# Cross-attention two batches at a time, with split sums of the query exponentials

## The chip, the cores and the metric

One core of one Trainium2 chip runs the whole kernel. Its engines are TensorE (PE in the profile, its weight loads PEld), VectorE (DVE), ScalarE (ACT), GpSimd (POOL) and SyncE (SP), which issues the DMAs. The metric is the device time of one launch in microseconds (us).

## What is computed

One decoder layer over x and ctx, both 32 x 64 x 512 (batch, channel, position), float32: a self-attention over the channels, a cross-attention, and a feed-forward net (FFN) whose operands are rounded to 8-bit floats in groups of 32, each followed by a layernorm over the 512 positions. The change is in the cross-attention:

```
def _L0_xattn_ref(q, k, v, Wq, Wk, Wv, Wo, bo, g):
    DIM = 64
    HEADS = 8
    DIM_HEAD = 64
    ...
    qh = jnp.einsum('bcn,oc->bon', q, Wq).reshape(b, HEADS, DIM_HEAD, -1)
    kh = jnp.einsum('bcn,oc->bon', k, Wk).reshape(b, HEADS, DIM_HEAD, -1)
    vh = jnp.einsum('bcn,oc->bon', v, Wv).reshape(b, HEADS, DIM_HEAD, -1)
    qh = jax.nn.softmax(qh, axis=-2) * SCALE
    kh = jax.nn.softmax(kh, axis=-1)
    context = jnp.einsum('bhdn,bhen->bhde', kh, vh)
    out = jnp.einsum('bhde,bhdn->bhen', context, qh)
    out = out.reshape(b, HIDDEN, -1)
    out = jnp.einsum('bcn,oc->bon', out, Wo) + bo[None, :, None]
    norm = jnp.maximum(jnp.sqrt(jnp.sum(out * out, axis=1, keepdims=True)), 1e-12)
    return out / norm * g * np.sqrt(DIM)
```

The layer is x1 = layernorm(x + self-attention), x2 = layernorm(x1 + xattn(x1, ctx, ctx)), out = layernorm(x2 + FFN(x2)).

## The kernel before

**Stages.** Up to 97 us the first FFN weights and x are loaded and rounded; up to 213.7 us the self-attention runs beside the rest of the weights; from 213.7 to 801.7 us the cross-attention; then the FFN. x lies in `xt` as 16 token tiles (t) of two batches: partitions 0 to 63 hold the channels of one batch, 64 to 127 those of the other.

**Cross-attention, one batch per slot.** `slot(b, par, t)` of each engine works on batch b = 2t + par; a turn t is two slots. All products are float32 with a contraction of 128 partitions, which TensorE does as two instructions each, except the query logits.
- Key logits: `logits` (L1204) multiplies `WkT[:, par]`, whose other 64 rows are zero, with the ctx tile `ctxs`: four products of 512 columns per batch into banks 0 and 1.
- Query logits (L1211): `keep_x1`, four DMAs (`load_x1d`), `high_x1` on ScalarE and `split_x1` (L465) on GpSimd make of x1 a pair of 16-bit halves stacked over 128 partitions (`x1p`); two 16-bit products of 512 columns per block i against `Wq2`, four blocks per batch, into banks 4 and 5.
- VectorE `maxima`: the row maximum of the key logits (L705), the maximum of each head's 64 query logits (L709) and the subtraction into `EQ` (L712). ScalarE `exps`: exp of the keys out of the bank (L960, with the running sum read by a second short instruction) and of the queries in place (L963). `q_sum` (L718) sums each head's 64 exponentials, 512 columns an instruction, eight a turn; `q_recs` (L722) inverts them; GpSimd `norm_p` (L475) multiplies.
- TensorE transposes the key exponentials (`transpose_k`, L1223) and the query ones (`transpose_p`, L1234), 16 blocks each per batch, through banks 2 and 3; ScalarE copies them out (L873) into `ET` and `PTs`.
- `a_product` (L1240): ctx times the key exponentials, four products of 512 columns. Only half of the result's rows belong to the batch; ScalarE copies these to `ATs`. Then four products with `Bs` (L1301) and `scale_g` (L742) give `GTs`; `y_product` (L1247) is 16 products of 64 columns with `PTs` as the weights.
- y, position by channel: `bias_y` (L726), the square (L487), `sum_y` (L732), the power -1/2 (L489) and the product (L490); `transpose_y` (L1255, L1270) and `add_y` (L749) bring it back to channel by position and add it to x1.

**Order.** Each engine runs one list written out by hand; semaphores order the lists. TensorE's list carries the logits of batch b + 1 between the transposes and products of batch b. Middle turns are loops.

## Time and profile before

| | us |
|---|---|
| median of 3 runs | 1008.78 |
| the three runs | 1013.59, 1008.78, 1008.75 |
| span of the profiled execution | 1010.8 |
| cross-attention, first key product to first FFN product | 588.0 |
| one turn (two batches) in its middle | 35.5 |
| busy in one such turn: TensorE, VectorE, ScalarE, GpSimd | 34.9, 30.7, 24.1, 17.5 |

No other duration is given for the profiled execution than its span, which stands 2.0 above the median. A row of the timeline is start, duration, engine, line, operation, output <- input, count, and in brackets the idle time before it and what ended it. With several instructions in a row, the duration runs from the first start to the last end. Instructions of an engine overlap a little, so that what counts along a chain is the distance of two starts.

### The profile page before, as it was taken

How to read it: one execution, taken by the hardware profiler on the slowest of the kernel's cores; microseconds unless marked ns; L12 is line 12 of the kernel's file. 1: busy time of each engine (PE TensorE's matmuls, PEld its weight loads, DVE VectorE, ACT ScalarE, POOL GpSimd, SP SyncE). 2: the span in 40 equal slices, each digit the busy share in tenths (PEclk: the TensorE clock that was granted, in tenths of full speed). 3: DMA queues.
4: the chain of work that ended last, by engine and by line, in shares of the span. 5: the costliest groups of instructions: out<-in, count | busy, mean ns of one | idle time of the engine just before them, and what ended most of it. 6: DMA issues, size and time to landing. Idle time of an engine off the chain costs nothing.

```text
span 1010.8 us, 17612 instructions
## 1 busy us (share of the span) xinstructions
PE 809.3 (80%) x5463; PEld 545.3 (54%) x5463; DVE 759.0 (75%) x1660; ACT 568.5 (56%) x1051; POOL 437.1 (43%) x491
## 2 busy tenths in 40 slices
PE   2115555548999999999999999999999867778873
PEld 2104555524767676676766667676667633333331
DVE  3766777748788888888888888888888266666663
ACT  1119777636666666766666676666667223333332
POOL 4423333313445455454545545454553334444443
PEclk7557676659999999999999999999999789999997
DMA  8993111101001101101100110110010000000000
GB/s 201 204 200 137 32 31 31 37 21 32 14 19 31 22 9 31 31 1 30 31 21 10 31 31 0 31 31 21 10 31 1 1 1 30 23 21 21 21 21 31
DMA packets 30372, 38.77 MB, mean 38 GB/s; under 512 B 4496, under 2 KB 16784, under 8 KB 30352
## 3 DMA queue, kind: packets, MB, share of 16 engines
q1 hardware_dynamic: 30352, 38.51, 15.9%
q8 instruction: 12, 0.20, 0.1%
q14 instruction: 8, 0.07, 0.0%
HBM read 25.92 MB, written 4.19 MB: 30 GB/s over the span
## 4 chain that ended last, share of the span: by engine, by line
PE 58%; issue 14%; POOL 8%; DMA 8%; DVE 6%; ACT 5%; SPq 1%; POOLq 0%; ACTq 0%; DVEq 0%
PE bank L1247 11%; PE bank L1204 11%; PE bank L1240 11%; PE bank L1223 5%; PE bank L1170 5%; PE bank L1211 5%; ACT big L873 4%; PE bank L1234 4%; DMA big<-in_ctx_dram 4%; POOL big L545 3%; POOL rstd L540 3%; DMA big<-in_L_ffn_w_down_dram 2%; PE bank L1301 2%; DMA big<-in_L_ffn_w_up_dram 2%; DVE big L565 1%
## 5 line engine op out<-in xcount | busy, mean ns | idle before, releaser
L873 ACT ACTIVATE big<-bank 128x512 f32<-128x512 f32 (+4 forms) x368 | 195.3, 588 | 53.1 <-PE bank L1223 31.5
L475 POOL TENSOR_TENSOR big<-big 128x512 f32<-128x512 f32 x128 | 131.5, 1057 | 81.1 <-DVE big L722 81.1
L1204 PE MATMUL bank<-big,WkT 128*128 128x512 f32 x256 | 136.2, 614 | 13.0 <-DMA big<-in_ctx_dram 8.8
L873 ACT ACTIVATE big<-big 32x256 f32<-32x256 f32 (+6 forms) x160 | 120.3, 772 | 15.6 <-DVE big L766 9.9
L963 ACT ACTIVATE big<-big,q_scales 128x512 f32<-128x512 f32 x128 | 92.4, 722 | 64.3 <-DVE big L712 64.3
L960 ACT ACTIVATE big<-bank,big 128x512 f32<-128x512 f32 x128 | 87.7, 685 | 68.6 <-DVE big L705 67.5
L1247 PEld LDWEIGHTS bank<-big 128*128 128x128 f32 x1024 | 120.6, 194 | 5.6 <-DVE big L742 1.2
L1247 PE MATMUL bank<-big 128*128 128x64 f32 x1024 | 119.4, 275 | 1.0 <-DVE big L742 1.0
L1240 PE MATMUL bank<-big 128*128 128x512 f32 x256 | 116.7, 598 | 0.5 <-ACT big L873 0.5
L718 DVE TENSOR_REDUCE big<-big 128x8 f32<-128x512 f32 x128 | 87.1, 680 | 25.7 <-ACT big L963 24.7
L705 DVE TENSOR_REDUCE big<-bank 128x1 f32<-128x512 f32 x128 | 88.2, 689 | 17.5 <-PE bank L1204 14.4
L1170 PE MATMUL bank<-big 128*128 128x128 f32 x256 | 55.9, 407 | 54.5 <-ACT big L873 54.5
L712 DVE TENSOR_TENSOR big<-bank,big 128x512 f32<-128x512 f32 x128 | 88.5, 691 | 6.9
L709 DVE TENSOR_REDUCE big<-bank 128x8 f32<-128x512 f32 x128 | 87.0, 680 | 7.4 <-PE bank L1211 7.4
L465 POOL TENSOR_TENSOR big<-big 64x512 f16<-64x512 f32 x32 | 37.0, 1157 | 116.1 <-ACT big L873 116.0
L1073 ACT ACTIVATE big<-big,rstd 128x512 f32<-128x512 f32 x16 | 13.0, 812 | 125.1 <-POOL big L541 125.1
L1211 PE MATMUL bank<-Wq,big 128*128 128x512 f16 x256 | 76.7, 381 | 7.2 <-POOL big L465 7.2
L1170 PEld LDWEIGHTS bank<-big 128*128 128x128 f32 x256 | 51.6, 308 | 56.6 <-issue 32.9
L545 POOL TENSOR_TENSOR big<-big 128x1376 f32<-128x1376 f32 x16 | 40.1, 2508 | 93.5 <-DVE big L569 93.5
L1240 PEld LDWEIGHTS bank<-big 128*128 128x128 f32 x256 | 47.4, 190 | 54.3 <-issue 41.6
L1234 PEld LDWEIGHTS bank<-ident,big 128*128 128x128 f32 x512 | 59.7, 140 | 23.5 <-issue 16.9
L565 DVE TENSOR_REDUCE big<-big 128x43 f32<-128x1376 f32 (+2 forms) x42 | 46.6, 1109 | 31.1 <-DMA big<-in_L_ffn_w_down_dram 21.6
(116 smaller groups left out, 1406.1 us busy)
## 6 DMA issues: line engine op xcount, KB each, us to landing
big<-big SPq DMA_DIRECT2D x64, 128.0 KB, 2.3
big<-in_x_dram SPq DMA_DIRECT2D x2, 2048.0 KB, 17.3
big<-in_x_dram SPq DMA_DIRECT2D x4, 1024.0 KB, 11.2
xt<-in_x_dram SPq DMA_DIRECT2D x1, 4096.0 KB, 15.0
big<-in_ctx_dram SPq DMA_DIRECT2D x16, 256.0 KB, 2.7
out_dram<-big SPq DMA_DIRECT2D x16, 256.0 KB, 2.0
big<-in_L_ffn_w_down_dram SPq DMA_DIRECT2D x4, 688.0 KB, 6.7
big<-in_L_ffn_w_gate_dram SPq DMA_DIRECT2D x10, 256.0 KB, 2.7
```

Of the source, the lines that this page charges most:

```text
L475: pool.tensor_tensor(e, e, r, ALU.mult).then_inc(s.p_ready, 1)
L705: dve.tensor_reduce(kneg[:, par, i:i + 1], bank[i % 2][:], X, ALU.max, negate=True).then_inc(s.k_max_ready, 1)
L712: dve.tensor_tensor(EQ[:, par, i].rearrange("p (h d) -> p h d", d=DH), q, qmax[:, par, i].unsqueeze(2).to_broadcast([P, HEADS, DH]), ALU.s ...
L873: return act.activation(dst, src, ACT.Copy)
L960: act.activation(EK[:, par, i], bank[i % 2][:], ACT.Exp, bias=kneg[:, par, i:i + 1], accum_out=ksum[:, par, i:i + 1]).then_inc(s.k_exp_don ...
L963: act.activation(EQ[:, par, i], EQ[:, par, i], ACT.Exp, scale=q_scales[:, 1:2]).then_inc(s.q_exp_done, 1)
L1170: last = pe.matmul(bank[4 + 2 * k + a][:, P * l:P * l + P], qs[:, k, CL // 2 * a + l].rearrange("m h c -> m (h c)"), pd[:, k, CL // 2 * a ...
L1204: pe.matmul(bank[i % 2][:], WkT[:, par, P * i:P * i + P], ctxs, start=True, stop=True).then_inc(s.klog_ready, 1)
L1211: last = pe.matmul(bank[4 + i % 2][:], x1p[:, par, P * i:P * i + P], Wq2[:, part], start=(part == 0), stop=(part == 1))
L1234: last = pe.transpose(bank[2 + j % 2][:, P * i:P * i + P], EQ[:, par, i, P * j:P * j + P], ident[:])
L1240: return pe.matmul(bank[6][:], ctxT[:, i], ET[:, i], start=(i == 0), stop=(i == NT - 1))
L1247: last = pe.matmul(bank[6][:, C * i:C * i + C], PTs[:, j, P * i:P * i + P], GTs[:, j], start=(j == 0), stop=(j == NJ - 1))
```

## The change

The cross-attention now works on both batches of a tile at once; per turn, with f = t + 1:
- Query logits are float32 products of x1 straight from `xt` with `WqT`; key logits use `WkT[rows]`. Each product contracts over 64 partitions only, and the two batches' products lie on different halves of the array's rows (`rows = slice(C * par, C * par + C)`). The 16-bit halves, the four DMAs, `keep_x1`, `high_x1`, `split_x1` and the scaling of Wq in the set-up go; the set-up issues two small DMAs more.
- `a_product` and `y_product` write 64 partitions each, one batch per half of the array's columns. `y_product` has `GTs` as the weights and 512 columns of `PTs`: 8 products of 512 columns for 32 of 64. `g_product` is 16 products of 64 x 64 with 64 columns a turn, for 8 of 64 x 128 with 128.
- y comes out channel by position. The bias is added by ScalarE, the square by GpSimd, the sum over channels by TensorE (`sum_squares`), the clamp by VectorE, the power by GpSimd; TensorE spreads it (`spread_rn`), VectorE multiplies (`norm_y`), GpSimd adds to x1 (`add_y`).
- `fold_p` on GpSimd adds the upper 32 columns of each head's exponentials to the lower 32, both batches at once, four a turn; VectorE's `q_sum` then sums 32 columns per head for both batches at once, four a turn instead of eight, with a reciprocal each.
- Key and query logits share banks 0 to 3, all transposes banks 4 and 5, and the phases are apart: all key logits of f (beside the query transposes of t), then `y_product(t)`, then all query logits of f with the key transposes and `a_product` of f. The turns are written out, not looped.

```diff
+            def fold_p(f, i):
+                pool.wait_ge(s.q_exp_done, 8 * f + 2 * i + 2)
+                if f or i >= 2:
+                    pool.wait_ge(s.q_rec_ready, 4 * f + i - 1)
+                e = EQ[:, :, i].rearrange("p b (h d) -> p b h d", d=DH)
+                pool.tensor_tensor(qfold[:, i % 2], e[:, :, :, 0:DH // 2], e[:, :, :, DH // 2:DH], ALU.add
+                                   ).then_inc(s.q_folded, 1)
...
-            def q_sum(b, par, i):
-                dve.wait_ge(s.q_exp_done, 4 * b + i + 1)
-                ch.link(dve.tensor_reduce(qsum[:, par, HEADS * i:HEADS * (i + 1)],
-                                          EQ[:, par, i].rearrange("p (h d) -> p h d", d=DH), X, ALU.add))
...
+            def q_sum(f, i):
+                if f:
+                    dve.wait_ge(s.p_ready, 8 * f - 6 + 2 * i)
+                dve.wait_ge(s.q_folded, 4 * f + i + 1)
+                ch.link(dve.tensor_reduce(qsum[:, i], qfold[:, i % 2], X, ALU.add))
+                dve.reciprocal(qsum[:, i], qsum[:, i]).then_inc(s.q_rec_ready, 1)
...
+            def scale_g(t):
+                dve.wait_ge(s.k_exp_done, 8 * t + 8)
+                ch.link(dve.reciprocal(krec, ksum))
+                if t:
+                    dve.wait_ge(s.y_ready, t)
+                for par in range(2):
+                    dve.wait_ge(s.gt_ready, 2 * t + par + 1)
...
+            dve.wait_ge(s.g8_ready, 1)
+            for t in range(-1, T):
+                f = t + 1
+                front, back = f < T, t >= 0
                 if front:
...
+                    k_max(f, 0)
+                if t >= 1:
+                    norm_y(t - 1)
+                if back:
+                    scale_g(t)
                 if front:
...
+                    k_max(f, 1)
+                    ln_stats(xt[:, f, :], s.x1_var)
+                    k_max(f, 2)
+                    ln_apply(f, s.x1_rstd, s.x1_ready)
+                if t >= 1:
+                    x2_stats(t - 1)
                 if front:
...
+                    k_max(f, 3)
+                if t >= 1:
+                    ln_apply(t - 1, s.x2_rstd, s.x2_ready)
                     scale_x(t - 1)
                 if front:
...
+                    q_shift(f, 0)
+                    q_shift(f, 1)
+                    q_sum(f, 0)
+                if back:
+                    clamp_ss(t)
                 if front:
...
+                    q_shift(f, 2)
+                    q_sum(f, 1)
+                if t >= 1:
                     quantize_x(t - 1)
...
                 if front:
...
+                    q_shift(f, 3)
+                    q_sum(f, 2)
+                    q_sum(f, 3)
...
+            def exp_k(f, i):
+                if f and i == 0:
+                    act.wait_ge(s.tr_ready, 16 * f - 8)
+                    act.wait_ge(s.gt_copied, 2 * f)
+                for par in range(2):
+                    act.wait_ge(s.k_max_ready, 8 * f + 2 * i + par + 1)
+                    act.activation(EK[:, par, i], bank[2 * (i % 2) + par][:], ACT.Exp, bias=kneg[:, par, i:i + 1],
+                                   accum_out=ksum[:, par, i:i + 1]).then_inc(s.k_exp_done, 1)
...
+            for t in range(-1, T):
+                f = t + 1
+                front, back = f < T, t >= 0
+                for i in range(NT):
+                    if front:
+                        exp_k(f, i)
+                    if back:
+                        copy_p(t, i // 2, i % 2)
                 if front:
...
+                    act.wait_ge(s.ctxT_ready, f + 1)
+                    if f:
+                        act.wait_ge(s.at_ready, f)
                     copy(ctxT, bank[7][:].rearrange("p (i c) -> p i c", i=NT)).then_inc(s.ctxT_copied, 1)
+                if back:
+                    act.wait_ge(s.y_ready, t + 1)
+                    if t:
+                        act.wait_ge(s.x2_added, t)
+                    act.activation(Ysb, bank[6][:], ACT.Identity, bias=bo2[:, 0:1]).then_inc(s.y_biased, 1)
                 if front:
...
+                    for i in range(NT):
+                        exp_q(f, i)
+                        copy_k(f, i)
+                    act.wait_ge(s.at_ready, f + 1)
+                    if f:
+                        act.wait_ge(s.gt_ready, 2 * f)
+                    copy(ATs, bank[6][:]).then_inc(s.at_copied, 1)
...
+            def a_product(f, i):
+                if i == 0:
+                    pe.wait_ge(s.ctxT_copied, f + 1)
+                    if f:
+                        pe.wait_ge(s.y_biased, f)
+                pe.wait_ge(s.tr_copied, 16 * f + 2 * i + 2)
+                for par in range(2):
+                    rows = slice(C * par, C * par + C)
+                    last = pe.matmul(bank[6][rows, :], ctxT[:, i, rows], ET[:, par, i],
+                                     start=(i == 0), stop=(i == NT - 1))
+                if i == NT - 1:
...
+            def g_product(t):
+                pe.wait_ge(s.at_copied, t + 1)
+                if t:
+                    pe.wait_ge(s.y_normed, t)
...
+            for t in range(-1, T):
+                f = t + 1
+                front, back = f < T, t >= 0
                 if front:
...
+                    k_logits(f, 0)
+                    k_logits(f, 1)
+                if back:
+                    transpose_p(t, 0, 0)
+                    g_product(t)
                 if front:
...
+                    k_logits(f, 2)
+                if back:
+                    transpose_p(t, 0, 1)
                 if front:
...
+                    k_logits(f, 3)
+                if back:
+                    transpose_p(t, 1, 0)
+                    transpose_p(t, 1, 1)
                 if front:
...
+                    transpose_ctx(f)
+                if back:
+                    y_product(t)
+                if front:
+                    q_logits(f, 0)
+                    q_logits(f, 1)
+                    transpose_k(f, 0)
+                    transpose_k(f, 1)
+                if back:
+                    sum_squares(t)
+                if front:
+                    q_logits(f, 2)
+                    transpose_k(f, 2)
+                    a_product(f, 0)
+                    q_logits(f, 3)
+                    transpose_k(f, 3)
+                    for i in range(1, NT):
+                        a_product(f, i)
+                if back:
+                    spread_rn(t)```

TensorE, in the middle of a turn. The names are those of the section above: L1204 and L1211 key and query logits, L1247 `y_product`, L1223 key transposes. Before:

```order
L1204 MATMUL bank<-big,WkT 128x512 [waits k_exp_done]
L1211 MATMUL bank<-Wq,big 128x512 [waits q_shifted]
L1211 MATMUL bank<-Wq,big 128x512
L1247 MATMUL bank<-big 128x64 [waits pqT_copied,gt_copied]
L1247 MATMUL bank<-big 128x64 x15
L1223 MATMUL bank<-ident,big 128x128 [waits kT_copied]
```

Now (L1111 query transposes, L1119 the transpose of ctx, L1154 `y_product`, L1089 query logits):

```order
L1111 MATMUL bank<-ident,big 128x128 [waits tr_copied]
L1111 MATMUL bank<-ident,big 128x128 x3
L1119 MATMUL bank<-ident,big 128x128 [waits gt_copied]
L1119 MATMUL bank<-ident,big 128x128 x3
L1154 MATMUL bank<-big 64x512 [waits tr_copied,gt_copied]
L1154 MATMUL bank<-big 64x512 x7
L1089 MATMUL bank<-WqT,xt 128x512 [waits k_exp_done,x1_ready]
L1089 MATMUL bank<-WqT,xt 128x512
L1089 MATMUL bank<-WqT,xt 128x512 [waits k_exp_done]
```

The query logits stood ahead of `y_product`, beside the key logits; they now stand behind it, and it waits for the copies of all query transposes of its turn.

ScalarE, from the first key exponential of a slot or turn. L960 and L963 are the exponentials of keys and queries, L873 the copies. Before:

```order
L960 ACTIVATE big<-bank,big 128x512 [waits gt_copied,kT_ready,k_max_ready]
L963 ACTIVATE big<-big,q_scales 128x512 [waits q_shifted]
L960 ACTIVATE big<-bank,big 128x512 [waits k_max_ready]
L963 ACTIVATE big<-big,q_scales 128x512 [waits q_shifted]
L873 ACTIVATE big<-bank 128x512 [waits kT_ready] x2
L960 ACTIVATE big<-bank,big 128x512 [waits k_max_ready]
```

Now (L875 and L881 the exponentials of keys and queries, L792 the copies, L916 the bias of y):

```order
L875 ACTIVATE big<-bank,big 128x512 [waits k_max_ready,gt_copied,tr_ready]
L875 ACTIVATE big<-bank,big 128x512 [waits k_max_ready]
L792 ACTIVATE big<-bank 128x512 [waits tr_ready] x2
L875 ACTIVATE big<-bank,big 128x512 [waits k_max_ready] x2
L792 ACTIVATE big<-bank 128x512 [waits tr_ready] x2
L792 ACTIVATE big<-bank 128x512 [waits at_ready,ctxT_ready]
L916 ACTIVATE big<-bank,bo 128x512 [waits y_ready]
L881 ACTIVATE big<-big 128x512 [waits q_shifted] x2
```

Key exponentials took turns with query exponentials; now eight key exponentials and eight copies come first (the second and third pairs of each alike), then the bias, then the query exponentials. `gt_copied` on the first one was that of the batch before the last; it is now that of the turn just behind.

VectorE, at the end of a turn and the start of the next. L705, L709, L712 as above, L718 and L722 the sums and their reciprocal, L742 `scale_g`. Before:

```order
L742 TENSOR_TENSOR big<-bank,big 64x256 [waits gt_ready,dve_chain]
L742 TENSOR_TENSOR big<-bank,big 64x256
L718 TENSOR_REDUCE big<-big 128x8 [waits q_exp_done]
L722 RECIPROCAL big<-big 128x32 [waits dve_chain]
L705 TENSOR_REDUCE big<-bank 128x1 [waits klog_ready]
L709 TENSOR_REDUCE big<-bank 128x8 [waits qlog_ready]
```

Now (L662 and L663 the sums and reciprocals, L644 the key maxima, L686 `norm_y`, L667 and L672 `scale_g`):

```order
L662 TENSOR_REDUCE big<-big 128x16 [waits q_folded,p_ready]
L663 RECIPROCAL big<-big 128x16 [waits dve_chain]
L644 TENSOR_REDUCE big<-bank 128x1 [waits klog_ready] x2
L686 SCALAR_TENSOR_TENSOR big<-big,g,bank 128x512 [waits y_squared,rn_spread]
L667 RECIPROCAL big<-big 128x8 [waits k_exp_done]
L672 TENSOR_TENSOR big<-bank,big 128x256 [waits gt_ready,dve_chain]
```

`scale_g` moved from ahead of the last sum to behind the first key maxima of the next turn and `norm_y`; the sum waits for GpSimd's fold, not for ScalarE.

## Rows read from the trace of the kernel before

**Rows 1.** The page: span and busy times, engine by engine.

```profile
span 1010.8 us, 17612 instructions
...
PE 809.3 (80%) x5463; PEld 545.3 (54%) x5463; DVE 759.0 (75%) x1660; ACT 568.5 (56%) x1051; POOL 437.1 (43%) x491
```

**Rows 2.** Stretches: busy us and instructions of each engine, then granted clock, DMA share, GB/s.

```profile
core 0: us, PE busy (x) PEld busy (x) DVE busy (x) ACT busy (x) POOL busy (x), PEclk, DMA share, GB/s
213.70:801.70 588.00, 563.94 (x3201) 388.61 (x3202) 486.83 (x1032) 384.80 (x753) 276.04 (x331) 0.98 0.09 21
497.25:532.75 35.50, 34.89 (x200) 24.15 (x201) 30.68 (x67) 24.07 (x48) 17.48 (x22) 1.00 0.09 22
```

**Rows 3.** Timeline of TensorE in one turn.

```profile
497.25 1.12 PE L1204 MATMUL bank<-big,WkT 128*128 128x512 f32 x2 [0.60 <-DMA big<-in_ctx_dram]
...
500.81 3.68 PE L1247 MATMUL bank<-big 128*128 128x64 f32 x32
...
509.93 1.04 PE L1234 MATMUL bank<-ident,big 128*128 128x128 f32 x8
510.81 1.02 PE L1204 MATMUL bank<-big,WkT 128*128 128x512 f32 x2
511.67 0.59 PE L1211 MATMUL bank<-Wq,big 128*128 128x512 f16 x2
512.10 1.04 PE L1234 MATMUL bank<-ident,big 128*128 128x128 f32 x8
513.06 1.16 PE L1301 MATMUL bank<-Bs,big 64*128 64x128 f32 x8
...
532.75 0.69 PE L1204 MATMUL bank<-big,WkT 128*128 128x512 f32 x1 [0.61 <-DMA big<-in_ctx_dram]
```

**Rows 4.** Timeline of VectorE in the same turn.

```profile
511.87 0.69 DVE L705 TENSOR_REDUCE big<-bank 128x1 f32<-128x512 f32 x1 [0.79 <-PE bank L1204]
512.47 0.68 DVE L709 TENSOR_REDUCE big<-bank 128x8 f32<-128x512 f32 x1
513.19 0.69 DVE L712 TENSOR_TENSOR big<-bank,big 128x512 f32<-128x512 f32 x1
513.81 0.64 DVE L574 TENSOR_SCALAR big<-big 128x512 fp8e4<-128x512 f32 x1
```

**Rows 5.** Timeline of ScalarE in the same turn.

```profile
496.97 1.06 ACT L873 ACTIVATE big<-bank 128x512 f32<-128x512 f32 x2
...
508.31 0.69 ACT L960 ACTIVATE big<-bank,big 128x512 f32<-128x512 f32 x1 [2.26 <-DVE big L705]
508.89 0.19 ACT L960 ACTIVATION_READ_ACCUMULATOR big<-bank,big 128x1 f32 x1
509.63 0.72 ACT L963 ACTIVATE big<-big,q_scales 128x512 f32<-128x512 f32 x1 [0.55 <-DVE big L712]
```

**Rows 6.** GpSimd in the same turn by line: count, busy us, mean ns, idle before.

```profile
L475 POOL TENSOR_TENSOR big<-big 128x512 f32<-128x512 f32 x8 | 8.2, 1057 | 4.6 <-DVE big L722 4.6
```

**Rows 7.** Products on parts of the array in the set-up and the self-attention, and their stretches.

```profile
23.52 1.61 PE L1123 MATMUL bank<-wg_area 64*64 64x64 f32 x32 [0.47 <-ACT wg_area L873]
...
110.20 0.86 PE L1159 MATMUL bank<-big 128*32 128x32 f32 x64
...
23.40:24.90 1.50, 1.38 (x32) 1.38 (x32) 0.00 (x0) 0.07 (x1) 0.00 (x0) 0.50 0.93 363
110.10:111.20 1.10, 0.96 (x66) 0.74 (x64) 1.01 (x4) 0.77 (x2) 1.10 (x1) 0.84 0.00 0
```

**Rows 8.** TensorE: first products of the cross-attention, and the first of the FFN.

```profile
213.68 2.04 PE L1204 MATMUL bank<-big,WkT 128*128 128x512 f32 x2 [1.31 <-ACT wuT L873]
...
801.67 1.78 PE L1335 MATMUL bank<-wg_area,big 128*128 128x480 bf16 x4 [0.69 <-ACT big L873]
```

**Rows 9.** TensorE in the FFN: a gap, and the stretch behind it.

```profile
869.52 0.89 PE L1348 MATMUL bank<-ident_bf,big 128*128 128x128 bf16 x11 [2.58 <-ACT big L1056]
...
872.00:875.00 3.00, 3.00 (x9) 1.06 (x7) 1.39 (x4) 0.15 (x1) 1.43 (x1) 0.50 0.00 0
```

713 lines of the change are left out of this document (252 added, 461 removed).

## The prediction

> **What bounds the kernel now.** First the page: the span is 1010.8 us, and TensorE is the busiest engine [rows 1]. Then the busy times by stretch: the cross-attention takes 588.0 us, TensorE is busy in 563.9 of them, and its granted clock is 0.98; in one turn of two batches in its middle TensorE is busy for 34.9 of 35.5 us, while VectorE has 30.7, ScalarE 24.1, GpSimd 17.5 [rows 2]. Then TensorE's timeline of that turn: the only idle time is 0.6 us at the turn's start, for the ctx tile [rows 3]. So today a turn is the sum of TensorE's instructions, and what the other engines gain is worth nothing while that stays. The question is what TensorE's sum becomes, and whether the new order still lets one engine work while the others do.
>
> **TensorE's sum.** A float32 product of 512 columns takes 0.86 us (510.81 to 511.67), two 16-bit ones 0.43 (511.67 to 512.10), eight transposes 0.88 (509.93 to 510.81), eight instructions of the present G 1.16, 32 instructions of the present `y_product` 3.68 [rows 3]. New per turn, if products run one after another: key logits 8 x 0.86 = 6.9 (as now), query logits 6.9 (now 8 x 0.43 = 3.4), `a_product` 6.9 (as now), `y_product` 6.9 (now 2 x 3.5 = 7.0), 64 transposes 7.0 (as now), ctx 0.4, G 1.8 to 2.6, `sum_squares` 0.9 and `spread_rn` 1.7 (8 and 16 instructions at the transposes' 0.11), less the 4 transposes of y. That is 40 us, 5 more than now.
>
> But all the 512-column products now come in pairs on disjoint halves of the array. No row shows such a pair. The nearest are short products on parts of it [rows 7]: 64 instructions of 32 columns on four column groups start within 0.86 - 0.20 = 0.66 us, 10.5 ns apart, where the 0.43 us of 512 columns gives 27 ns for 32 alone; and 32 instructions of 64 x 64 and 64 columns take 1.6 us at half clock, 42 ns apart where 107 would be one after another. Both overlap by about 2.5. I take it that a pair costs as one (0.86); the bounds are 1.29 (the second starts when the first's first half is done) and 1.73 (none). With 0.86 the sum is 4 x 3.45 + 7.0 + 0.4 + 0.9 (G: the 1.6 at half clock, halved) + 0.9 + 0.9 = 24 us. The Trainium skill ("TensorE: Matmul & The Clock Gate", Part 3, packing small matmuls) states the same side: different tile positions run concurrently, four row tiles with 512 columns 3.07 times as fast; by that figure, an estimate, a pair is nearer 0.9 than 1.7. Rows 7 agree in kind.
>
> **VectorE, GpSimd, ScalarE.** VectorE loses four of eight sums of 512 columns (4 x 0.6, each step being 0.60 to 0.72 from start to start [rows 4]), the bias, one of two sums of y and the small memsets: 30.7 falls to about 27. GpSimd gains four folds at 1.05 us, the price of its 512-column product [rows 6], +4.2, loses the splits, and stays near 20. ScalarE stays at 22 to 24. So no engine needs more than 27 us, and by busy time alone the turn would fall. The halved sums are taken at nothing: they lie on an engine with 8 us to spare in the new turn.
>
> **What the new order makes of the turn.** The logits no longer cross the slots: the turn has a key phase and a query phase that hand over to each other, as the order of the three engines shows. I follow the chain round one turn, each step from start to start. A product pair is read 1.06 us after its start (510.81 to 511.87), a maximum takes 0.60, the query maximum 0.72 and its subtraction 0.62 (511.87, 512.47, 513.19, 513.81) [rows 3, 4]; a key exponential 0.58 with a read of 0.19 behind it, so 0.77 to 0.80 (at least 0.70, as neighbours overlap by 0.1); a query exponential 0.72, copies 0.5 apart [rows 5].
> 1. From the turn's first key product to ScalarE's first key exponential, which now waits for `scale_g` of the turn behind: 1.08 + two maxima 1.2 + `norm_y` 0.8 (G may not overwrite bank 7 before it) + G 1.0 + `scale_g` 0.5 = 4.6.
> 2. ScalarE's block, eight key exponentials and eight copies, because `y_product` waits for the last copy: 8 x 0.8 + 8 x 0.51 + 0.1 = 10.6. TensorE and VectorE mostly wait here.
> 3. `y_product`, which stands ahead of the query logits: 4 x 0.86 = 3.5.
> 4. From the first query product to the third: 1.08 + two maxima and subtractions 2.7, the exponential 0.7, two copies 1.15, four transposes 0.44, `sum_squares` 0.9 = 7.0.
> 5. From there to the next turn: 1.08, `q_shift` 2 2.64, a sum and its reciprocal 0.84, the rounding of x 1.26, `q_shift` 3 2.75, exponential and copies 1.8, the last part of `a_product` 0.87, `spread_rn` 0.9 = 12.15.
> Together 37.85 us. Behind VectorE's last subtraction the fold, the sum and `norm_p` of GpSimd (1.05 + 0.9 + 4 x 1.02) run beside TensorE's 7 us of transposes, products and the next key logits, and come in within a microsecond of them; the fold costs 0.2 a turn if it takes 1.3 instead of 1.05.
>
> Three corrections. The exponentials may be 0.1 shorter each: -0.4 as the middle. Where the tiling changes there is a gap of 0.09 us (512.10 + 0.88 to 513.06) [rows 3]; some seven such changes lie on the chain: +0.6. TensorE now idles several times a turn for 1.5 to 2.6 us, and behind a gap of 2.58 us in the FFN the granted clock of a stretch is 0.50, the lower level of 1.2 GHz [rows 9]. About 10.8 us of the chain are TensorE's; all at the lower level would cost +10.8. I take +0.55, a twentieth. **A turn of 38.6 us.** The Trainium skill ("TensorEngine Tiling (Array Packing)", Tiling Modes, key properties) says that a change of the tiling mode drains TensorE; that speaks against this order, which changes it some 17 times a turn, and the 0.09 us is what the trace shows of it.
>
> **The sum.** The first turn has a front only (23.3 us from key product to key product), the second is short (37.3), 13 more are full, and the last with the back behind it is 55.9: 116.5 + 13 x 38.6 = 618.3 us, and 1.3 to the first FFN product (the transposes and copy of x, as today). Today it is 801.67 - 213.68 = 588.0 [rows 8]. +31.6. The set-up loses VectorE's scaling of Wq but has two more DMAs ahead of the weights, and the first FFN turn waits for the last norm: -1 and +1. 1010.8 + 31.6 = 1042.4 by the profiled execution, which stands 2.0 above the median of the runs: **1040 us**.
>
> **Rivals.**
> - *TensorE's clock falls in the gaps* (slower still). For it: the gaps and the row of the FFN [rows 9]. Against: no gap exceeds 2.6, and today's attention holds 0.98. A quarter of TensorE's 10.8 us at the lower level: +2.7 a turn, 41.3, +75 to 85 us, about 1085. Chance 0.16.
> - *The pairs do not overlap* (the speed-up of the array is absent for long products): steps 1, 3, 4, 5 grow, the walk gives 45.9 a turn, 736 + 1.3 - 588 = +149, about 1157. Rows 7 speak against it. Chance 0.06. If they overlap by halves (1.29), the turn is 39.5 and the time 1067; that lies in my own case.
> - *The chain is shorter than I add it up* (faster). Its point of balance is a turn of 36.6, since the first turn no longer waits for the DMAs of x1's halves. ScalarE's block at 0.70 an exponential takes off 0.4 more, and 0.05 less at each of some 35 hand-overs 1.75: 38.6 - 0.55 - 0.4 - 1.75 = 35.9, 11 us less than now, about 997. For it: no engine is busy for over 27 us, so nothing but the waits holds the turn. Against: the hand-overs were read from rows. Chance 0.20, of which 0.03 for a turn at VectorE's 27 to 30 (900 to 940).
> - *The split sums matter, or don't happen as said*: if the fold and sum were in the chain the turn would gain or lose only 0.2 to 0.7; no case of its own.
>
> **How the numbers follow.** Forecast 0.50 (1018 to 1070), clock 0.16, no overlap 0.06, faster by over 0.5% 0.20, within 0.5% of today 0.08 (turns of 36.3 to 36.9). 0.5% is about what a measurement of this kernel can tell from no change. Slower: 0.50 + 0.16 + 0.06 = 0.72. The range is 995 to 1100: it leaves out no overlap, a few hundredths of the clock case above, and half of the faster case.
>
> **What would show it.** In the profile after: a turn of 37.3 to 39.5; TensorE busy for about two thirds of it, with idle time ahead of `y_product`, of the third key product and of the key transposes, ended by ScalarE; VectorE idle for some 7 us ahead of the first query maximum, ended by TensorE; ScalarE's eight exponentials and copies back to back over 10 us; two starts of a product pair a few tens of nanoseconds apart. Wrong would be: starts 0.86 apart (no overlap), 0.43 apart (half), a granted clock below 0.9 in the turns (the clock), or VectorE without its long gap (the chain is shorter).

## The result, and the profile after

| kernel | median, us | runs | ratio to the kernel before | 95% interval |
|---|---|---|---|---|
| before | 1011.18 | 1013.59, 1008.78, 1008.75, 1014.03 | | |
| after | 1063.98 | 1061.74, 1057.08, 1066.22, 1070.14 | 1.0519 | 1.0463 to 1.0575 |

Medians are over all runs of a kernel, ratios and intervals over the faster ones where its runs fall into two groups. The changed kernel is 5.2% slower: 53 us, where 29 to 32 were forecast. The rows of the page after (span; busy time; in 40 slices TensorE's busy tenths and granted clock; the chain of waits by engine):

```profile
span 1059.9 us, 15236 instructions
...
PE 732.5 (69%) x5249; PEld 421.5 (40%) x5264; DVE 681.0 (64%) x1396; ACT 505.3 (48%) x985; POOL 473.0 (45%) x474
...
PE   2115555587877777787787787787777778777774
...
PEclk9998767679899889889889899999998879999896
...
PE 32%; DVE 24%; ACT 16%; issue 14%; POOL 8%; DMA 4%; ACTq 1%; SPq 1%; POOLq 0%; DVEq 0%
```

Against [rows 1] TensorE does 77 us less and the kernel takes 49 more. The loss lies in the cross-attention. Its stretch now, beside [rows 2], and three of its turns (us, busy time of each engine, granted clock, DMA share, GB/s):

```profile
215.97:854.35 638.38, 491.46 (x3013) 265.38 (x3013) 407.98 (x775) 323.00 (x690) 314.56 (x317) 0.90 0.02 7
281.16:318.59 37.43, 28.62 (x191) 15.25 (x189) 25.11 (x49) 19.93 (x43) 19.46 (x21) 0.95 0.03 8
317.61:354.70 37.09, 27.29 (x191) 14.42 (x189) 24.99 (x50) 19.93 (x43) 19.32 (x21) 1.00 0.02 8
521.24:562.37 41.13, 31.81 (x191) 17.64 (x189) 26.32 (x49) 20.27 (x43) 20.19 (x21) 0.88 0.03 7
```

638.4 for 588.0 us is +50.4; the set-up is 2.3 longer and the FFN 3.6 shorter. The turns differ, though their instructions are the same. By TensorE's `spread_rn` the fourteen full turns take 37.4, 37.1, 42.5, 41.0, 41.0, 41.0, 41.1, 41.3, 38.0, 39.0, 37.6, 37.7, 37.8 and 41.7 us, at granted clocks of 0.95, 1.00, 0.84, 0.88 (five times), 0.96, 0.91, 0.95 (three times) and 0.85. Only the second has the full clock throughout, and seven of the fourteen lie below 0.9. TensorE in the first of the turns shown above; its gaps stand in brackets:

```profile
281.16 1.99 PE L1077 MATMUL bank<-big,WkT 64*128 64x512 f32 x8
283.08 1.09 PE L1111 MATMUL bank<-ident,big 128*128 128x128 f32 x8
284.41 0.69 PE L1143 MATMUL bank<-Bs,big 64*64 64x64 f32 x32 [0.24 <-DVE big L686]
287.58 1.13 PE L1077 MATMUL bank<-big,WkT 64*128 64x512 f32 x4 [2.48 <-ACT big L875]
288.64 1.09 PE L1111 MATMUL bank<-ident,big 128*128 128x128 f32 x8
...
295.58 3.65 PE L1154 MATMUL bank<-big 128*64 128x512 f32 x16 [1.31 <-ACT big L792]
299.16 1.99 PE L1089 MATMUL bank<-WqT,xt 64*128 64x512 f32 x8
...
304.26 1.14 PE L1100 MATMUL bank<-ident,big 128*128 128x128 f32 x8 [2.09 <-ACT big L792]
...
306.12 1.60 PE L1089 MATMUL bank<-WqT,xt 64*128 64x512 f32 x4
...
316.70 1.08 PE L1130 MATMUL bank<-big 128*64 128x512 f32 x4 [1.89 <-ACT big L792]
317.61 1.04 PE L1169 MATMUL bank<-ident,big 128*64 128x128 f32 x16
318.59 1.99 PE L1077 MATMUL bank<-big,WkT 64*128 64x512 f32 x8
```

Two pairs of 512-column products (x8, as each product is two instructions) start 1.92 us before what follows them (281.16 to 283.08), and one pair alone 1.06 us (287.58 to 288.64). So a further pair adds 0.86, the time of a single product [rows 3]: the pairs overlap fully. The 0.20 us that each group has beside its pairs lies at its two ends, where the tiling of the array changes. One row each of ScalarE and VectorE shows who waits for whom, the first key exponential (L875) for `scale_g` and the first query maximum (L651) for the query logits:

```profile
286.08 0.69 ACT L875 ACTIVATE big<-bank,big 128x512 f32<-128x512 f32 x1 [5.08 <-DVE big L672]
```

```profile
300.32 0.69 DVE L651 TENSOR_REDUCE big<-bank 128x8 f32<-128x512 f32 x1 [6.04 <-PE bank L1089]
```

Now the long turn, in rows of 3 us around its losses (same columns as above; the granted clock is the third number from the end):

```profile
524.24:527.24 3.00, 0.71 (x33) 0.59 (x32) 2.13 (x7) 1.08 (x3) 1.27 (x1) 1.00 0.00 0
527.24:530.24 3.00, 2.58 (x11) 1.67 (x12) 2.09 (x6) 2.90 (x9) 0.74 (x2) 0.71 0.00 0
...
542.24:545.24 3.00, 0.97 (x8) 0.73 (x8) 2.93 (x5) 1.74 (x4) 0.40 (x1) 1.00 0.00 0
545.24:548.24 3.00, 2.94 (x16) 2.94 (x16) 2.31 (x5) 2.48 (x6) 1.62 (x2) 0.56 0.00 0
548.24:551.24 3.00, 3.00 (x10) 1.49 (x11) 0.83 (x2) 0.14 (x1) 3.00 (x4) 0.50 0.00 0
```

Twice in this turn TensorE has little work (0.71 and 0.97 us in a row of 3), and as it has work again its clock falls to or towards the lower level of 1.2 GHz. The work there is on the chain. The clock does not fall behind every gap: the longest one of this turn, 2.95 us ahead of the last part of `a_product` (560.48), is followed by a clock of 1.00. The same anchors as the prediction's five steps, in both turns:

| step | forecast | turn at 281 | turn at 521 |
|---|---|---|---|
| 1: first key product to first key exponential | 4.6 | 4.92 | 4.92 |
| 2: ScalarE's block, to `y_product` | 10.6 | 9.50 | 10.46 |
| 3: `y_product` | 3.5 | 3.58 | 3.58 |
| 4: first to third query product | 7.0 | 6.96 | 8.27 |
| 5: to the next turn | 12.15 | 12.47 | 13.90 |
| sum | 37.85 | 37.43 | 41.13 |

Step 5 of the long turn holds one loss more, on VectorE. The rounding of x2 (L706) takes 0.69 us in the turn at 281 and 1.64 here, where it falls beside GpSimd's third fold (L436):

```profile
311.68 0.69 DVE L706 TENSOR_TENSOR big<-big 128x512 bf16<-128x512 fp8e4 x1
...
554.51 1.64 DVE L706 TENSOR_TENSOR big<-big 128x512 bf16<-128x512 fp8e4 x1
```

```profile
310.67 1.66 POOL L463 TENSOR_TENSOR big<-big,minus_half 128x8 f32<-128x8 f32 x1
...
554.06 1.54 POOL L436 TENSOR_TENSOR big<-big 128x512 f32<-128x512 f32 x1 [0.70 <-ACT big L881]
```

In the turn at 281 GpSimd is in its small power instruction then, and a fold takes 1.27 us. The Trainium skill ("SBUF — State Buffer", SBUF: two separate sides) says that a VectorE instruction with two SBUF inputs and a GpSimd instruction that reads SBUF exclude each other on a shared port pair, one waiting until the other is done. L706 has two SBUF inputs and the fold reads SBUF, and the trace agrees: L706 ends 0.55 us behind the fold (556.15 and 555.60), though it began in the fold's course, and grows by 0.95. What made the fold itself take 1.54 instead of 1.27 isn't shown.

### The profile page after: what moved, and what is told of

Same layout as the page of the kernel before. It is cut to its first block, busy times and chain, and to the rows that moved or that the text cites. A ratio compares the mean times of both kernels' runs of the same rounds, so it can differ in the third digit from the quotient of the medians.

```text
span 1059.9 us, 15236 instructions
## 1 busy us (share of the span) xinstructions
PE 732.5 (69%) x5249; PEld 421.5 (40%) x5264; DVE 681.0 (64%) x1396; ACT 505.3 (48%) x985; POOL 473.0 (45%) x474
## 2 busy tenths in 40 slices
PE   2115555587877777787787787787777778777774
## 4 chain that ended last, share of the span: by engine, by line
PE 32%; DVE 24%; ACT 16%; issue 14%; POOL 8%; DMA 4%; ACTq 1%; SPq 1%; POOLq 0%; DVEq 0%
ACT big L792 10%; DVE big L651 6%; PE bank L1154 5%; PE bank L1040 5%; PE bank L1077 5%; ACT big L875 5%; PE bank L1089 4%; DVE big L654 4%; DVE big L527 3%; POOL big L510 3%; POOL rstd L505 3%; DMA big<-in_L_ffn_w_down_dram 2%; PE bank L1111 2%; PE bank L1100 2%; PE bank L1130 2%
## 5 line engine op out<-in xcount | busy, mean ns | idle before, releaser
L792 ACT ACTIVATE big<-bank 128x512 f32<-128x512 f32 (+3 forms) x352 | 188.5, 600 | 39.1 <-PE bank L1130 19.9
L651 DVE TENSOR_REDUCE big<-bank 128x8 f32<-128x512 f32 x128 | 87.3, 682 | 113.9 <-PE bank L1089 113.9
L881 ACT ACTIVATE big<-big 128x512 f32<-128x512 f32 x128 | 80.6, 630 | 142.8 <-DVE big L654 142.8
L445 POOL TENSOR_TENSOR big<-big 128x512 f32<-128x512 f32 x128 | 133.2, 1068 | 0.0
L875 ACT ACTIVATE big<-bank,big 128x512 f32<-128x512 f32 x128 | 87.8, 705 | 83.7 <-DVE big L672 78.4
L436 POOL TENSOR_TENSOR big<-big 128x512 f32<-128x512 f32 x64 | 83.7, 1308 | 88.5 <-ACT big L881 88.5
L644 DVE TENSOR_REDUCE big<-bank 128x1 f32<-128x512 f32 x128 | 82.0, 682 | 51.5 <-PE bank L1077 51.5
L1100 PE MATMUL bank<-ident,big 128*128 128x128 f32 x512 | 86.7, 323 | 35.7 <-ACT big L792 35.3
L1077 PE MATMUL bank<-big,WkT 64*128 64x512 f32 x256 | 79.6, 726 | 40.0 <-ACT big L875 38.7
L1100 PEld LDWEIGHTS bank<-ident,big 128*128 128x128 f32 x512 | 66.7, 163 | 87.4 <-ACT big L792 61.5
L1130 PE MATMUL bank<-big 128*64 128x512 f32 x256 | 67.8, 630 | 36.8 <-ACT big L792 36.8
L792 ACT ACTIVATE big<-big 32x256 f32<-32x256 f32 (+4 forms) x112 | 90.3, 834 | 1.1
L1111 PE MATMUL bank<-ident,big 128*128 128x128 f32 x512 | 78.4, 301 | 7.2 <-ACT big L792 6.8
L1111 PEld LDWEIGHTS bank<-ident,big 128*128 128x128 f32 x512 | 60.7, 152 | 51.8 <-ACT big L792 23.1
L1089 PE MATMUL bank<-WqT,xt 64*128 64x512 f32 x256 | 79.1, 718 | 0.3 <-ACT big L875 0.3
L457 POOL TENSOR_TENSOR big<-big 128x512 f32<-128x512 f32 x16 | 16.6, 1038 | 134.9 <-ACT big L916 134.9
L1040 PEld LDWEIGHTS bank<-big 128*128 128x128 f32 x256 | 52.8, 314 | 56.5 <-issue 40.1
L1154 PE MATMUL bank<-big 128*64 128x512 f32 x256 | 58.5, 597 | 20.4 <-ACT big L792 20.4
```

Of the source, the lines that this page charges most:

```text
L445: pool.tensor_tensor(e, e, r, ALU.mult).then_inc(s.p_ready, 1)
L651: ch.link(dve.tensor_reduce(qmax[:, i, par], q, X, ALU.max))
L792: return act.activation(dst, src, ACT.Copy)
L875: act.activation(EK[:, par, i], bank[2 * (i % 2) + par][:], ACT.Exp, bias=kneg[:, par, i:i + 1], accum_out=ksum[:, par, i:i + 1]).then_inc ...
L1040: last = pe.matmul(bank[4 + 2 * k + a][:, P * l:P * l + P], qs[:, k, CL // 2 * a + l].rearrange("m h c -> m (h c)"), pd[:, k, CL // 2 * a ...
L1077: pe.matmul(bank[2 * (i % 2) + par][:], WkT[rows, P * i:P * i + P], ctxs[rows, f % 2], start=True, stop=True).then_inc(s.klog_ready, 1)
```

## The experiments

The theory after this reading: a turn is the chain of hand-overs, some 37 us at full clock (the turn at 317.61 above), and the falling clock adds some 2.5 on the average. Rivals: the chain is the wrong one (shortening a hand-over then brings nothing); the clock is a companion of the slow turns and not their cause; the split sums cost or gain what the words of the change suggest. To compare, one number was read in each trace: the fourteen full turns, from the first to the fifteenth `spread_rn`. The first row is the kernel after, 39.6 us a turn; the rows of the others follow where they are discussed.

```profile
280.19:834.52 554.33, 425.71 (x2634) 230.43 (x2632) 360.54 (x688) 281.38 (x602) 278.96 (x282) 0.91 0.02 7
```

**The fold undone.** GpSimd adds nothing, and VectorE sums 64 columns.

```diff
-                dve.wait_ge(s.q_folded, 4 * f + i + 1)
-                ch.link(dve.tensor_reduce(qsum[:, i], qfold[:, i % 2], X, ALU.add))
+                dve.wait_ge(s.q_exp_done, 8 * f + 2 * i + 2)
+                e = EQ[:, :, i].rearrange("p b (h d) -> p b h d", d=DH)
+                ch.link(dve.tensor_reduce(qsum[:, i], e, X, ALU.add))
...
```

> The fold of GpSimd is taken out again: VectorE sums all 64 columns of each head for both batches, 1024 columns an instruction. Theory (a chain of hand-overs round the turn; the split sums lie beside it): the second sum of a turn stands on the chain and grows from 0.7 to about 1.25 us, +0.5 a turn; VectorE's last rounding instruction, 1.64 us beside GpSimd's fold in the turns of 41 us and 0.69 in those of 37.5, may go back to 0.69. 1050 to 1072 us. Rival (the fold and its extra hand-over, or its load on GpSimd, make the kernel slow): at least 1.5 us less a turn, below 1040.

Measured: 1080.42 us, ratio 1.0703 (1.066 to 1.0746); turns of 38.9 to 42.7. That is 16 us slower than after and above every expectation. The split sums are not the loss; they are a gain. Whether the unsteady clock makes it larger (1.2 us a turn between these two traces) can't be told from one trace each; a later run measures them at a held clock.

**Query logits ahead of `y_product`.** Steps 3 and 4 of the chain: VectorE gets its first query maxima while TensorE is in `y_product`.

```diff
+                if front:
+                    q_logits(f, 0)
+                    q_logits(f, 1)
                 if back:
                     y_product(t)
                 if front:
-                    q_logits(f, 0)
-                    q_logits(f, 1)
                     transpose_k(f, 0)
```

> TensorE's first two groups of query logits stand ahead of y_product instead of behind it; nothing else changes. Theory: y_product's 3.6 us leave the chain for VectorE's first maxima, and ScalarE's first query exponential comes some 1.5 to 2 us earlier: a turn shorter by 2.1 us (walk of the chain), about 1030, 1015 to 1045 with the clock. Rival (TensorE's own work sets the turn): no change, 1055 or more.

Measured: 1012.43 us, ratio 0.996 (0.9914 to 1.0007), no difference from the kernel before that can be told: 52 us, the whole loss, came back for two lines in another place. That is a little below the expected 1015 to 1045.

```profile
273.52:783.10 509.58, 408.42 (x2634) 214.41 (x2632) 356.36 (x687) 277.41 (x602) 273.73 (x281) 0.94 0.03 7
```

The turn falls by 3.2 to 36.4 us. That is more than the 2.1 expected of the hand-over itself; the granted clock rose from 0.91 to 0.94 as well. The clock was under-estimated in the gain as in the loss.

**The reciprocals of the key sums at the turn's end.** In the kernel after, VectorE inverts the key sums at the next turn's start, so ScalarE's next key exponentials, whose running sums go to the same place, wait for `scale_g` (step 1). Here the reciprocal stands at the turn's end with a semaphore of its own.

```diff
-                dve.wait_ge(s.k_exp_done, 8 * t + 8)
-                ch.link(dve.reciprocal(krec, ksum))
+                dve.wait_ge(s.krec_ready, t + 1)
...
+                    dve.wait_ge(s.k_exp_done, 8 * f + 8)
+                    if f:
+                        dve.wait_ge(s.gt_copied, 2 * f)
+                    dve.reciprocal(krec, ksum).then_inc(s.krec_ready, 1)
...
-                    act.wait_ge(s.gt_copied, 2 * f)
+                    act.wait_ge(s.krec_ready, f)
```

> The reciprocal of the key sums is taken at the end of the turn, so that ScalarE's first key exponential of the next turn waits for it and no longer for scale_g. Theory: step 1 of the chain, 4.6 us from the first key product to the first key exponential, falls to about 2; ScalarE's block starts some 3 us earlier, of which 1.7 to 3 stay: 1015 to 1040. Rival (ScalarE's block is not on the chain): no change, 1055 or more.

Measured: 1034.76 us, ratio 1.0241 (1.02 to 1.0282): inside the expectation. Where the clock is 1.00 a turn takes 35.2 us, 1.8 less than after; in between lie turns of 40.2 at 0.87. Both hand-overs are on the chain. The mean of the fourteen turns fell by 1.5 only, to 38.1, with the clock at 0.91 as in the kernel after.

**TensorE kept busy.** Thirteen products of 256 columns that nobody reads, at four places where TensorE stood idle; nothing else moves.

```diff
+            def keep_busy(b, n, semaphore, value):
+                pe.wait_ge(semaphore, value)
+                for _ in range(n):
+                    pe.matmul(bank[b][:, 0:256], ident[:], ident[:].unsqueeze(1).to_broadcast([P, 2, P]),
+                              start=True, stop=True)
...
+                if front and back:
+                    keep_busy(6, 3, s.gt_copied, 2 * t + 2)
...
+                        if back and i == NT - 1:
+                            keep_busy(7, 4, s.y_ss, t + 1)
```

> After's kernel with 13 products a turn (256 columns of the identity, 0.43 us each) put into TensorE's idle time at four places, into banks that nobody reads; work is only added. Theory (the turns of 41 us are those in which TensorE's clock falls to 1.2 GHz in the gaps): granted clock above 0.95 in the turns, all turns 37.4 to 38.5, 1030 to 1045 us. Rival (the long turns come from another cause, such as VectorE and GpSimd colliding): the turns of 41 us stay, 1058 or more.

Measured: 1022.34 us, ratio 1.0119 (1.0088 to 1.0151).

```profile
275.72:793.50 517.78, 464.96 (x2999) 265.66 (x2996) 350.87 (x685) 279.40 (x602) 271.24 (x280) 1.00 0.03 7
```

TensorE does 39 us *more* work in these turns and they are 36.5 us shorter, each 37.0 at a clock of 1.00. The kernel after takes as long, 37.1, in its one turn at full clock, where nothing was added; so the unread products change the turn by nothing but the clock that they hold. The time is below the expected 1030 to 1045, since no turn is longer than the shortest expected. So the clock costs 42 of the 53 us, with what follows from it, and the other 11 are what the chain costs at full clock: a turn takes 37.0 us against the 35.5 of the kernel before, and the whole cross-attention 600.2 against 588.0, as what lies outside the fourteen turns is some 9 us shorter. VectorE's busy time falls by 9.7 although its list is untouched, 6.6 of it in L706, which no longer meets a fold (14 times 692 ns on the average, 1166 in the kernel after).

**Both moves.** The second and the third edit together.

> Both orders of before at once: first query logits ahead of y_product, and the reciprocal of the key sums at the end of the turn. Theory (chain of hand-overs): the two lie on different steps of the chain, so they add up, some 3.8 us a turn off at full clock (33.5 us a turn), and the granted clock again below 1 in some turns: 960 to 1000 us. Rival (an engine's work becomes the bound at about 35 us): no faster than the better of the two, 1000 to 1015.

Measured: 980.83 us, ratio 0.9652 (0.9596 to 0.9708), the first version that beats the kernel before. Turns take 33.0 us at a clock of 1.00 and up to 37.1 at 0.87; the profiled execution was the slowest of the four (991.69), so its mean of 35.0 is above that of the others. At full clock the reciprocals give 1.8 and the query logits, on top of them, 2.2 (37.0, 35.2, 33.0). The two add up as expected, and the result is inside the 960 to 1000.

**Both moves, and TensorE kept busy at four places** (twelve products).

> The same with 12 unread products a turn in TensorE's idle time (256 columns of the identity, 0.43 us each). Theory: clock 1.00 in all turns, a turn of 33.5 to 34 us, 15 x 3 to 3.5 us less than the kernel with the unread products alone (1022): 965 to 980. Rival (the unread products now stand in the way, since the gaps are shorter): slower than the same kernel without them.

Measured: 1000.06 us, ratio 0.986 (0.9816 to 0.9903). Missed: the clock is 1.00, yet every turn takes 35.4. TensorE shows why:

```profile
566.03 1.56 PE L1181 MATMUL bank<-ident 128*128 128x256 f32 x6 [0.95 <-DVE big L672]
567.53 1.13 PE L1081 MATMUL bank<-big,WkT 64*128 64x512 f32 x4
...
575.67 1.13 PE L1181 MATMUL bank<-ident 128*128 128x256 f32 x4
576.74 3.65 PE L1158 MATMUL bank<-big 128*64 128x512 f32 x16
```

The unread products (L1181) wait for VectorE's `scale_g` (L672), and the third key product stands behind them in the queue; with both moves it no longer had to wait for that. It comes 6.39 us after the turn's first (561.14) instead of 3.87, and the first query product 1.3 us later than with both moves alone; the two unread products ahead of `y_product` (575.67), another place where TensorE no longer waits, add the other 1.1. A filler sits on the chain as soon as the wait that it filled is gone.

**Both moves, and unread products at two places only**, two behind the bias of y and four behind `y_ss`, where idle time was left.

> The run with both moves (query logits ahead of the y product, reciprocals of the key sums at the turn's end), with six unread 256-column products on TensorE at two places only: two behind the bias of y, four behind the root of the squares, both at points where TensorE stood idle in that run's trace. Its turns were 33.0 us at a granted clock of 1.00 and 37.1 at 0.87. Theory (the clock is what stretches its turns, and the twelve unread products of the run before it lay partly on the chain, ahead of the third key product, which these six don't): every turn at 1.00 and 33.0 to 34.0 us, 16 turns some 30 us shorter than with the clock unsteady, so 955 to 975 us. Rival (any product in the gaps comes into the chain's way, or the clock falls all the same): 980 us or more, turns of 35 us or at clocks under 0.95.

Measured: 962.66 us, ratio 0.9505 (0.946 to 0.955), all turns 33.0 to 33.1:

```profile
272.50:735.07 462.57, 417.76 (x2803) 228.64 (x2801) 352.38 (x685) 276.28 (x602) 272.92 (x280) 1.00 0.03 8
```

**TensorE kept busy at two of the four places** in the kernel after.

> Unread products at two of the four places alone (three ahead of the third key products, four between the first and second key transposes); the gaps ahead of y_product (1.3 us) and of the last part of a_product (1.9 to 3.0) stay. Theory (every gap counts for the clock by its length): a part of the 42 us, 1025 to 1050, granted clock between 0.94 and 0.98 in the turns. Rival (the last gap alone lets the clock fall): 1055 or more.

Measured: 1031.72 us, ratio 1.0172 (1.0122 to 1.0223), turns of 37.0 to 38.6 at clocks of 1.00 to 0.96. Two filled gaps, those ahead of the third key product and behind the first key transposes, give back most of it: 32 of 42 us. The length of one gap doesn't decide it: that of 2.48 us ahead of the third key product is followed by 1.00 in the turn at 281 and by 0.71 in the turn at 521.

**The fold undone at a held clock.** The first edit together with the thirteen unread products.

> The split sums undone (VectorE sums 64 columns, no fold) with 13 unread products a turn as in the kernel of 1022 us; the clock is thus held and only the sums differ. Theory (the longer sums stand on the chain between q_shift 2 and q_shift 3 and ahead of the last norm_p): turns alike, 0.5 to 1.5 us longer than 37.0, 1030 to 1046. Rival (undoing the split costs time only through the clock): within 5 us of 1022.

Measured: 1031.92 us, ratio 1.0183 (1.0136 to 1.0229), all turns 37.5.

```profile
277.03:802.35 525.32, 464.94 (x2999) 265.69 (x2997) 379.49 (x686) 279.43 (x602) 209.48 (x225) 1.00 0.02 7
```

Against the run with the fold, VectorE has 28.6 us more in fourteen turns (four sums of 1.20 instead of 0.68), GpSimd 61.8 less, and a turn is 0.5 us longer, 7.5 us over the fourteen; the medians differ by 9.6, the ratios by 0.6% (the two were measured beside different runs of the kernel before). The split sums are worth 0.5 us a turn where the order gives GpSimd room.

**The kernel before with the fold alone.** One batch and one tile at a time, in the old order.

```diff
+            def fold_p(b, par, i):
+                pool.wait_ge(s.q_exp_done, 4 * b + i + 1)
+                e = EQ[:, par, i].rearrange("p (h d) -> p h d", d=DH)
+                pool.tensor_tensor(qfold[:, par, i], e[:, :, 0:DH // 2], e[:, :, DH // 2:DH], ALU.add
+                                   ).then_inc(s.q_folded, 1)
...
-                dve.wait_ge(s.q_exp_done, 4 * b + i + 1)
+                dve.wait_ge(s.q_folded, 4 * b + i + 1)
...
```

> The kernel before with one part of the change alone: GpSimd adds the 32-column halves of each head's query exponentials, one batch and one tile at a time, and VectorE sums 32 columns. Nothing else moves. Theory (a slot of the kernel before is bound by TensorE, rows 7, and what VectorE gains and GpSimd loses lies in their idle time; GpSimd's four folds of some 0.65 us each stand in front of its products with the reciprocals): within 1% of the kernel before, 1002 to 1022 us. Rival A (the split sum is a gain by itself also there): under 1000 us. Rival B (GpSimd's folds delay the high and low parts and the normalised exponentials that TensorE waits for): 1025 us or more.

That TensorE bounds a slot stands in [rows 2], not in rows 7. Measured: 1051.72 us, ratio 1.0388 (1.0339 to 1.0436). The theory, that it changes nothing, was wrong; the time is that of rival B. The chain of waits by engine, and VectorE's sums, GpSimd's folds and ScalarE's key exponentials by line, with the sums and the exponentials of the kernel before behind them:

```profile
POOL 30%; issue 29%; PE 10%; ACT 10%; DVE 9%; DMA 8%; SPq 3%; POOLq 1%; ACTq 0%; DVEq 0%
...
L739 DVE TENSOR_REDUCE big<-big 128x8 f32<-128x256 f32 x128 | 53.7, 420 | 122.6 <-POOL big L474 122.1
L474 POOL TENSOR_TENSOR big<-big 128x256 f32<-128x256 f32 x128 | 94.7, 740 | 69.5 <-ACT big L983 69.5
...
L980 ACT ACTIVATE big<-bank,big 128x512 f32<-128x512 f32 x128 | 87.7, 685 | 131.1 <-DVE big L726 130.6
```

```profile
L718 DVE TENSOR_REDUCE big<-big 128x8 f32<-128x512 f32 x128 | 87.1, 680 | 25.7 <-ACT big L963 24.7
...
L960 ACT ACTIVATE big<-bank,big 128x512 f32<-128x512 f32 x128 | 87.7, 685 | 68.6 <-DVE big L705 67.5
```

Each sum is 0.26 us shorter (420 ns against 680), 33 us in all. But VectorE now waits 122 us for the folds, at a place in its queue where the sums waited 26 before. What stands behind them in the queue comes later, the key maxima too: ScalarE's key exponentials wait 131 us for these, 69 before, and TensorE for ScalarE. The chain runs through GpSimd's list, whose folds stand between its products with the reciprocals, the square of y and the low halves of x1. So rival B's time came by another road in the main: the folds hold up VectorE's queue more than GpSimd's own results. One turn:

```profile
499.99:538.08 38.09, 35.88 (x201) 23.80 (x200) 28.72 (x66) 23.61 (x48) 23.22 (x29) 1.00 0.09 21
```

38.1 us against 35.5 [rows 2], at a clock of 1.00. Whether the folds and sums, placed elsewhere in the two lists, would win that back wasn't tried.

**More hand-overs shortened**, by five more moves on top of both: the first key transposes also ahead of `y_product`, the third query product ahead of `sum_squares`, the third `q_shift` ahead of `clamp_ss`, ScalarE's first query exponential and first copy ahead of the bias of y, and the first fold ahead of the square. TensorE's part of the edit, against the run with both moves:

```diff
                     q_logits(f, 0)
                     q_logits(f, 1)
+                    transpose_k(f, 0)
                 if back:
                     y_product(t)
                 if front:
-                    transpose_k(f, 0)
                     transpose_k(f, 1)
+                    q_logits(f, 2)
                 if back:
                     sum_squares(t)
                 if front:
-                    q_logits(f, 2)
```

> The run with both moves, and four hand-overs of the turn shortened further: the first transpose of the key exponentials also ahead of the y product; the third query product ahead of the sums of squares; on ScalarE the first query exponential and the first copy ahead of the bias of y; on VectorE the shift of the third query maxima ahead of the sums of the tile before; on GpSimd the first fold ahead of the square of y. Theory (a turn is the chain of hand-overs, and each of these is a step of it): 31.0 to 32.5 us a turn where the clock is 1.00, 1 to 2 us less than with both moves alone; with the clock unsteady as there, 940 to 975 us. Rival A (the turn is then bound by the sum of TensorE's own work, some 29 us at full clock, and the later bias of y delays the A product): turns of 33 us or more at 1.00, 975 us or more. Rival B (shorter gaps keep the clock at 1.00 as well): all turns near 32, 925 to 945 us.

Measured: 944.37 us, ratio 0.932 (0.9276 to 0.9365). Inside the expected 940 to 975. Turns take 31.4 us, every third one or so 32.8 at a clock of 0.95. How the 1.6 us divide among the five moves wasn't taken apart. The fourteen turns, and two that follow each other with the gap at the end of each:

```profile
271.06:716.38 445.32, 384.37 (x2634) 201.99 (x2632) 352.32 (x687) 279.07 (x602) 271.74 (x281) 0.98 0.03 8
302.45:333.85 31.40, 26.99 (x191) 14.19 (x188) 25.14 (x50) 19.93 (x43) 19.40 (x21) 1.00 0.04 9
333.85:366.62 32.77, 28.61 (x191) 14.96 (x189) 25.17 (x50) 19.93 (x43) 19.40 (x21) 0.95 0.02 9
```

```profile
332.94 1.08 PE L1138 MATMUL bank<-big 128*64 128x512 f32 x4 [2.58 <-ACT big L797]
...
365.71 1.08 PE L1138 MATMUL bank<-big 128*64 128x512 f32 x4 [2.57 <-ACT big L797]
```

Both turns have the same three gaps of over 0.6 us (0.94, 0.65 and 2.58). Behind the one at 332.94 the clock falls for a while, which is the 0.95 of the turn that begins there; behind its like at 365.71 the next turn runs at 1.00.

**The same with six unread products** at the two places.

> The run with the four further hand-overs shortened, and six unread 256-column products of TensorE at two places: two behind the bias of y, ahead of the third transpose of the key exponentials, four behind the root of the squares, ahead of the last A product. Theory (the chain at a held clock): all turns 31.5 to 33 us at 1.00, 925 to 955 us. Rival (with so little idle time left, unread products cost what they take, 0.11 us each at full clock and their waits): equal to or slower than the run without them, by up to 20 us.

Measured: 939.9 us, ratio 0.9289 (0.9241 to 0.9337), all turns 31.4 to 31.5 at 1.00. The interval overlaps that of the run without them, so no gain is shown by the times; the two traces differ by 4.6 us over the fourteen turns (445.32 against 440.69), but the clock had little left to give. An unread product takes 0.5 us (four in 1.99), not the 0.11 of the expectation. It is the fastest kernel of the study, 6.6 to 7.6% below the kernel before and 12% below the one after.

## Why the prediction was right, and where its size was not

**Slower, for the reason given: shown.** TensorE's sum fell from 34.9 us a turn to 27.3 where the clock is 1.00 (24 forecast; that sum left out the changes of tiling), VectorE's to 25 and ScalarE's to 20 (27 and 22 to 24 forecast), and no engine is busy for over 32 of 41; the turn is a chain through all engines. Two of its hand-overs, undone one by one, gave 2.2 and 1.8 us a turn at a clock of 1.00.

**The pairs overlap.** A further pair adds 0.86 us, as taken (1.92 for two, 1.06 for one), and the changes of tiling add the 0.2 beside a group of pairs. The rival without overlap is out, and so is the half overlap of 1.29.

**The five steps, without the clock.** The turn at full clock is 37.0 us (TensorE kept busy), where the forecast without its 0.55 for the clock was 38.05. In that run the five steps take 4.92, 9.51, 3.58, 6.96 and 12.01. The forecast was 1.05 too long, by step 2: ScalarE's eight exponentials and copies took 9.5 us instead of 10.6, since neighbours overlap (two exponentials start 0.66 to 0.68 apart, where 0.8 was taken). Steps 1, 3, 4 and 5 came within 0.32. VectorE's gap ahead of the query maxima is 6.0 us (forecast 7).

**The term that was mis-sized is the clock.** "I take +0.55, a twentieth" stands in the prediction for what the gaps do to TensorE's 10.8 us on the chain. Measured: 39.6 - 37.0 = 2.6 us a turn, the size of the rival (2.7) that had a chance of 0.16; and by the prediction's own sign for that rival, a clock below 0.9 in the turns, it came true in seven of fourteen. That the time still fell between 1018 and 1070 is in part luck, as the two errors stand against each other: 14 turns x (2.05 - 1.05) = +14 us, and the first two turns, 65.2 us instead of 60.6, are the 19 us between the forecast 619.6 and the measured 638.4. With the steps as long as forecast, 1.05 us more a turn, and the clock as it was, the time would have been some 15 us longer than 1064, above 1070. The argument against the rival was that today's attention holds 0.98 and that no gap exceeds 2.6 us. The first is true but doesn't bear on it: today's turn has one gap of 0.6, and the new one has five of over 0.6 us. The second holds at full clock (2.48 is the longest gap), not in the long turns, where the slower work makes one of 2.96. The row of the FFN [rows 9] showed the case, and was given a twentieth.

**The loss of clock spreads.** The forecast priced TensorE's own work only. In the long turns L706 takes 0.95 us more as well, because it meets the third fold. That VectorE and GpSimd hold each other up was in none of the steps.

**The split sums.** "Taken at nothing" in the busy sum, and 0.2 to 0.7 a turn if on the chain: measured 0.5. The fold took 1.27 to 1.31 us for the 1.05 taken.

**The ends.** The first two turns took 25.4 and 39.8 us (23.3 and 37.3 forecast) at clocks of 0.83 and 0.87; with TensorE kept busy they take 25.5 and 36.9, so the excess of the second is the clock again, and that of the first is not explained. The first key product came 2.3 us later (forecast 1 earlier), the FFN was 3.6 us shorter (forecast 1 longer); neither was followed up.

## What to carry over

When a new order takes work off a busy engine and turns its sum into a chain of hand-overs, write down the chain, and then price TensorE's part of it at both clock levels: four gaps of 1.3 to 3.0 us in a turn cost here 42 of 1064 us through the clock, and shortening the hand-overs gave that back along with the steps. Before the bound is accepted, look for products that wait in the queue behind work that nobody needs yet: two such moves turned +5.2% into -3.5%, five more into -6.8%. And a reduction made shorter by a helper on another engine is only shorter where its queue doesn't stand waiting for the helper.

## What the runs showed of the hardware

- Products that nobody reads, six or thirteen a turn of some 0.5 us each, held the granted clock at 1.00 in all turns, where it had been 0.91 to 0.94 in the mean, and made the kernel 1.5 to 4% faster; placed ahead of a product on the chain, the same fillers cost 2.4 us a turn.
- Two float32 products of 512 columns on disjoint halves of the array's rows take 0.86 us together, as long as one (two pairs in 1.92, one in 1.06), and so do two on halves of its columns (four pairs of `y_product` in 3.58). Between products of different tiling stands about 0.1 us more.
- A VectorE instruction of 0.69 us with two SBUF inputs took 1.64 beside a GpSimd addition that reads SBUF. How the waits divide between the two engines was not measured by itself.
- What decides the clock in a given turn stays open: with five more moves the same gaps went with a clock of 1.00 in two turns and 0.95 in the third, a gap of 2.95 us was followed by 1.00 and one of 2.09 in the same turn by 0.56, and no run here told the cases apart.
